# First layer of a conditioned Mamba block: places inside a chunk and halved pairs placed anew

## What is computed

```python
xn = layernorm(x) * (1 + scale) + shift            # scale, shift, gate from silu(cond) @ ada_w.T + ada_b
x_in, z = split(xn @ in_proj_w.T)                  # 1024 channels each
u = silu(causal_conv(x_in, 4 taps) + conv_b)
dt_r, B, C = split(u @ x_proj_w.T)                 # 64, 16, 16
dt = softplus(dt_r @ dt_proj_w.T + dt_proj_b)
h[t] = h[t-1] * exp(dt[t] * A) + dt[t] * u[t] * B[t]      # per channel, 16 states
y[t] = sum over states of h[t] * C[t]  +  u[t] * D
x1 = x + gate * ((y * silu(z)) @ out_proj_w.T)
```

## Time and profile before

| | us |
|---|---|
| median of 3 runs | 2549.21 (2546.92 to 2552.84) |
| the profiled execution, its time | 2547.39 |
| the profiled execution, its span | 2545.6 |
| mean granted clock of TensorE | 0.941 of full |
| first scan to last scan of the first layer | 81.7 to 2044.7 |

### The profile page before, as it was taken

The page is one execution under the profiler, slowest core; times in us unless marked ns, Lnnn a source line. Parts: engine busy times, 40 slices in busy tenths (PEclk is TensorE's granted clock), DMA queues, the critical chain, the costliest instruction groups (busy, mean ns, idle before and its releaser), DMA issues. The chain is left out here.

```text
span 2545.6 us, 23866 instructions
## 1 busy us (share of the span) xinstructions
PE 2240.3 (88%) x6820; PEld 1160.5 (46%) x6820; DVE 2241.4 (88%) x2508; ACT 1591.7 (63%) x3049; POOL 1879.0 (74%) x1217
## 2 busy tenths in 40 slices
PE   8798879887987898899878988898877899999999
PEld 3233334333433343334333433333333369988887
DVE  3789999999999999999999999999999976676656
ACT  3557756765676567657765776577555445556645
POOL 0699988988898889889998888899886742222325
PEclk9899989998998899899989998999898999999999
DMA  5510131032104100412041004110410211112113
GB/s 195 214 58 25 63 129 37 26 110 81 38 28 141 52 34 25 150 41 71 21 150 50 29 21 154 38 33 17 158 46 1 81 63 32 32 40 68 50 43 124
DMA packets 78049, 176.09 MB, mean 69 GB/s; under 512 B 7453, under 2 KB 10781, under 8 KB 77918
## 3 DMA queue, kind: packets, MB, share of 16 engines
q1 hardware_dynamic: 77918, 174.56, 19.8%
HBM read 157.23 MB, written 17.30 MB: 69 GB/s over the span
## 5 line engine op out<-in xcount | busy, mean ns | idle before, releaser
L1311 POOL TENSOR_TENSOR arena<-arena 128x1024 f32<-128x1024 f32 x512 | 1200.9, 2359 | 106.0 <-ACT arena L535 79.9
L929 DVE TENSOR_TENSOR_SCAN arena<-ps,arena 128x512 f32<-128x512 f32 x1024 | 1253.2, 1253 | 2.0 <-ACT ps L535 2.0
L535 ACT ACTIVATE ps<-arena 128x512 f32<-128x512 f32 x1088 | 730.5, 683 | 528.7 <-DVE arena L929 497.4
L300 PE MATMUL ps<-arena,keep 128*128 128x512 f32 x1712 | 867.8, 640 | 135.4 <-POOL arena L1311 69.6
L917 DVE TENSOR_TENSOR arena<-ps,arena 128x1024 f32<-128x1024 f32 x512 | 615.4, 1202 | 53.0 <-PE ps L300 39.7
L300 PEld LDWEIGHTS ps<-arena,keep 128*128 128x128 f32 x1712 | 340.0, 204 | 615.6 <-issue 386.8
L247 PE MATMUL ps<-arena 128*128 128x512 f32 x1024 | 464.6, 598 | 3.0 <-ACT arena L535 3.0
L247 PEld LDWEIGHTS ps<-arena 128*128 128x128 f32 x1024 | 197.8, 194 | 258.0 <-issue 255.0
L1276 POOL TENSOR_TENSOR arena<-arena 128x512 f32<-128x512 f32 x168 | 213.6, 1271 | 46.6 <-ACT arena L535 38.2
L286 PE MATMUL ps<-arena 128*128 128x512 f32 x512 | 232.9, 596 | 1.0 <-issue 1.0
L1316 POOL TENSOR_TENSOR arena<-arena 128x512 f32<-128x512 f32 x168 | 213.9, 1273 | 13.2
(11 more groups left out here) (130 smaller groups left out, 2607.7 us busy)
## 6 DMA issues: line engine op xcount, KB each, us to landing
arena<-scr_bc SPq DMA_DIRECT2D x128, 512.0 KB, 7.2
arena<-in_inT SPq DMA_DIRECT2D x128, 256.0 KB, 2.6
arena<-in_x SPq DMA_DIRECT2D x17, 512.0 KB, 3.7
scr_x<-arena SPq DMA_DIRECT2D x32, 256.0 KB, 2.0
arena_b<-scr_x SPq DMA_DIRECT2D x16, 512.0 KB, 3.6
arena_c<-scr_x SPq DMA_DIRECT2D x32, 256.0 KB, 2.8
out<-arena_c SPq DMA_DIRECT2D x32, 256.0 KB, 2.0
arena<-in_x SPq DMA_DIRECT2D x30, 256.0 KB, 3.2
```

What stands on the lines that cost most here:

```text
L300: last = e.matmul(YP, ident, hb[G % R][:, i, :], start=False, stop=(g == NG - 1 and i == n - 1))
L535: return e.activation(o_, i_, f, **kw)
L929: e.tensor_tensor_scan(H, DA[s % 4], H, h0, MUL, ADD).then_inc(v_sc)
L1311: m_ = e.tensor_tensor(H, H, Ct[:, GN * g:GN * g + GN, :], MUL)
```

## The change

It moves entries in the tables and writes the table of halved pairs anew; no step's own code changes. 168 pairs were halved; now it is 20 in each chunk but in unit 39 none, 157 in all. In a middle chunk: the output products go from slots 7, 8 of unit 0, 0, 3 of unit 1 and 3, 5, 9, 10 of unit 2 to slots 4, 8, 15 of unit 0, 5 of unit 1 and 3, 5, 9, 12 of unit 2. The input products x1 to x7 move by one to five slots, and their evacuations and taps with them. The second half of the norm's steps goes later, except RS, which goes earlier. `softplus` goes from slot 7 to 8, one `SILU` from (5, 11) to (5, 14), another, with `proj`, one slot later, and two z products later.

```diff
@@ -148,32 +148,32 @@
 
         after = lambda k, n: ((16 * k[0] + k[1] + n) // 16, (k[1] + n) % 16)
 
-        AT = {"dt": 4, "soft": 7, "add": 8, "du": 6, "copy": 13, "yf": 7, "proj": (6, 14), "xdbl": (7, 5)}
-        XMM = {(2, 12): 0, (3, 2): 1, (3, 15): 2, (4, 2): 3, (4, 11): 4, (5, 0): 5, (5, 15): 6, (6, 6): 7}
+        AT = {"dt": 4, "soft": 8, "add": 8, "du": 6, "copy": 13, "yf": 7, "proj": (6, 15), "xdbl": (7, 5)}
+        XMM = {(2, 12): 0, (3, 5): 1, (4, 1): 2, (4, 5): 3, (4, 13): 4, (5, 1): 5, (6, 0): 6, (6, 7): 7}
         XEV = {after(k, 4): i for k, i in XMM.items()}
         TAP = {after(k, (2, 3, 4)[w]): (i, 2 - w) for k, i in XMM.items() for w in range(3)}
-        SILU = {(3, 14): (0, 2), (5, 11): (2, 5), (6, 14): (5, 8)}
-
-        ZMM = {(1, 8): 1, (1, 10): 2, (3, 8): 1, (3, 10): 2, (5, 5): 1, (5, 10): 2, (7, 8): 1, (7, 12): 2}
-        ZSILU = {(1, 14): (1, 2), (3, 14): (1, 2), (5, 14): (1, 2), (7, 14): (1, 2)}
-
-        STATS = {(0, 3): 0, (1, 0): 1}
-        RS = {(0, 3): 0, (1, 6): 1}
-        NORM = {(0, 8): 0, (1, 11): 1}
-        NTR = {(0, 13): 0, (1, 13): 1}
-        NEV = {(0, 14): 0, (1, 15): 1}
-
-        OUTM = {(0, 7): 0, (0, 8): 4, (1, 0): 8, (1, 3): 12, (2, 3): 16, (2, 5): 20, (2, 9): 24, (2, 10): 28}
-        OUTA = {(0, 12): 0, (1, 3): 1, (2, 8): 2, (3, 1): 3}
-
-        HALF = {0: (2, 3, 4, 6), 1: (0, 1, 2, 3, 5), 2: (0, 3, 5), 3: (), 4: (4, 6), 5: (), 6: (5,), 7: (0, 2, 4, 5, 6, 7)}
+        SILU = {(3, 14): (0, 2), (5, 14): (2, 5), (6, 15): (5, 8)}
+
+        ZMM = {(1, 8): 1, (1, 10): 2, (3, 8): 1, (3, 10): 2, (5, 5): 1, (5, 11): 2, (7, 11): 1, (7, 12): 2}
+        ZSILU = {(1, 15): (1, 2), (3, 14): (1, 2), (5, 14): (1, 2), (7, 14): (1, 2)}
+
+        STATS = {(0, 0): 0, (1, 2): 1}
+        RS = {(0, 2): 0, (0, 15): 1}
+        NORM = {(0, 10): 0, (1, 5): 1}
+        NTR = {(0, 13): 0, (2, 1): 1}
+        NEV = {(0, 14): 0, (2, 3): 1}
+
+        OUTM = {(0, 4): 0, (0, 8): 4, (0, 15): 8, (1, 5): 12, (2, 3): 16, (2, 5): 20, (2, 9): 24, (2, 12): 28}
+        OUTA = {(0, 12): 0, (1, 6): 1, (2, 8): 2, (3, 1): 3}
+
+        HALF = {0: (5,), 1: (0, 1, 2, 3), 2: (0, 1, 2, 3), 3: (0, 1, 2), 4: (4,), 5: (3,), 6: (1, 5, 7), 7: (0, 2, 4)}
 
         CPART = {after(k, n): (i, n) for i, k in enumerate([(0, 6), (1, 6), (2, 2)]) for n in range(4)}
         CROW, CCOL, CEND = {(0, 11): 0, (1, 11): 1, (2, 7): 2}, {(1, 14): 1, (2, 9): 2}, {(2, 1): 1, (2, 12): 2}
 
-        GATE = {(1, 8): (0, 0), (1, 12): (0, 1), (2, 0): (0, 2), (2, 4): (0, 3), (39, 2): (1, 0), (39, 5): (1, 1),
-                (39, 8): (1, 2), (39, 11): (1, 3)}
-        halved = lambda U, g: g in HALF[U % 8]
+        GATE = {(1, 8): (0, 0), (1, 12): (0, 1), (2, 0): (0, 2), (2, 4): (0, 3), (39, 0): (1, 0), (39, 7): (1, 1),
+                (39, 9): (1, 2), (39, 15): (1, 3)}
+        halved = lambda U, g: g in HALF[U % 8] and U != 39
 
         WSEQ = [(0, i) for i in range(10)]
         for U in range(NU):
```

## The result

The changed kernel takes 2492.1 us (median of 4 runs, 2490.4 to 2493.1) against 2548.1 us for the kernel before on the same chip (median of 4, 2544.2 to 2552.8). The ratio is 0.978, 95% interval 0.976 to 0.980: 56 us faster. The profiled execution took 2492.05 us, its span is 2490.3.

A forecast was written before the change was run, and what follows sets the result against it. VectorE bounds the kernel; reordering can win only its 73.1 us idle in the first layer. Terms sum to -40 us: 2547.4 - 40 + 1.8 = 2509 us, range 2494 to 2543; the forecast case spans 2493 to 2524.

The forecast's parts named there:

- (4,6) and (5,6): Slot 6 of units 4 and 5: sums with 1.1 and 1.3 us to spare stall in a chunk or two, +2 us.
- unit 0, `expand` and `x1_add` at slot 12: Unit 0: both waits go at either clock, 2.3 us in each of 7 chunks, taken as -15 us.
- gates, units 39 to 41: Chunk 5: GpSimd has 29.5 us of work beside the gate products instead of 37.1, so waits go, -6 us.
- unit 6: TensorE's hole before `y_fin` shrinks from 3.8 us to about 2; if the clock stays high, -9 us.
- ScalarE's group: Unit 5: a silu moved to slot 14 delays the exps behind it, 0.3 us in 7 chunks, +2 us.
- seam: Before layer two's transposes: GpSimd ends 4 us sooner, TensorE has 3 matmuls more; 0 to 2 us, taken as -1.
- Unit 0 is the same: Unit 0: as in unit 6, TensorE idles (4.87 us), its sums run slowly, slot 12's `expand` idles 1.37 us.
- Rival C: Granted clock stays as it is, savings come back at other pairs, only the gates gain: 2543 us; chance 0.13.
- Rival A: Clock falls at a 3.1 us hole ending unit 3; units 4 and 5 lose 56 us: 2565 us; chance 0.09.
- Rival B: Clock falls at some of rival A's places or unit 6 stays low: 22 us gained, 2527 us; chance 0.20.
- Rival D: ScalarE's group exposed, 1.5 us in 7 chunks: 2518 us; with extra switch time 2536 us; chance 0.03 for both.
- the remaining 22 us: VectorE's idle time in units 3, 4, 5, 7 of seven chunks: half goes, -11 us, since spare is 1 us.

The follow-up runs named there:

- e2_places_only: The changed kernel with the old list of halved pairs in every unit, 39 included: 2517.6 us, ratio 0.989 to the kernel before.
- e5_fill016: The kernel before with four unread matmuls at slot 5 of units 0, 1 and 6: 2535.2 us, ratio 0.995.
- e10_fill1: The changed kernel with four unread matmuls at slot 5 of unit 1: 2494.5 us, ratio 0.979 to the kernel before.

## Why the prediction was right in sign and too small

The terms of the sum, us, by the two traces. The rows down to (4,6) and (5,6) are VectorE's idle time between the first and last scan, the unit rows without chunk 0:

| Step | forecast | measured |
|---|---|---|
| unit 0, `expand` and `x1_add` at slot 12 | -15 | -16.1 |
| unit 0, `expand` at slot 10 | 0 | -1.2 |
| gates, units 39 to 41 | -6 | -5.6 |
| unit 6 | -9 | -8.3 |
| units 3, 4, 5, 7 | -11 | -17.4 |
| a wait for a load in unit 1, and idle times under 0.15 us | 0 | -1.7 |
| chunk 0 | -2 | -4.5 |
| ScalarE's group | +2 | +1.3 |
| (4,6) and (5,6) | +2 | +1.4 |
| seam | -1 | -2.0 |
| overlap of VectorE's instructions | 0 | -3.9 |
| time to the first scan | 0 | +2.7 |
| sum (profiled spans 2545.6 and 2490.3) | -40 | -55.3 |

**Mechanism.** For unit 6 the chain from hole to clock to late sum to `expand` is shown, by unit 6 filled in the old order, and by chunk 2 against chunk 3 within the changed kernel. For unit 0 the order is what counts: its waits at slot 12 are gone in `e2_places_only` with the clock at 0.81 to 0.89, as the prediction said they would at either clock. "Unit 0 is the same" as unit 6 was wrong: the hole of 4.87 us ended at GpSimd's halving and not at `y_fin`. Rival C is out: the clock of unit 0 is 1.00 in chunk 3 and 0.94 to 1.00 in chunks 1 to 7. Rival A did not occur: the hole at the end of unit 3 is 1.7 us, not the 3.1 that I followed, the clock stayed high, and (4,6) and (5,6) cost 1.4 us outside chunk 0. Rival B is out, since the clock stayed high at all its places in most chunks (unit 6 kept it low in two). Rival D is out at both its prices: 1.8 us in all, chunk 0 included, in place of 10 or more. Nothing here shows the drain of about 1380 ns that the Trainium skill, ScalarE: Activation LUTs, section What ACT_TABLE_LOAD costs, adds to a switch: by it the moved group would have been exposed in every chunk, and the scan at (6,1) waits in three only. The load itself took 1.28 us, against the 1283 ns of the Trainium skill's page.

**The step that failed** is "the remaining 22 us ...: half, -11". By the traces these waits were 20.5 us and fell to 3.1, so -17.4; the other 1.8 of the 22 lay elsewhere. I took half because the spare was 1 us and I didn't follow these chains one by one. Most behaved all or none: (5,10) went from 8.0 to 0.9 us, `y_fin` at (4,7) and (5,7) from 7.7 to 0, `expand` at (4,0) from 2.5 to 0 (chunk 0 left out); only (7,4) kept 1.2 of its 1.6, and 0.9 came new at (4,10). For unit 5 my own numbers had said so: pair 7 is ready 2.5 us sooner against a wait of 0.9. That should have been taken whole.

**The low end of the range** was a wrong sum besides. "All but chunk 0's idle gone" is 73.1 - 14.5 = 58.6 us and not 56, so 2491 and not 2493.

**Terms that were missing.** Idle time was not "all that reordering can win". VectorE's busy time in the layer fell by 3.9 us (1889.9 to 1886.0) with the same instructions. In both kernels a scan that follows a scan without a wait starts 1190 ns after it, less than the recorded duration: neighbours overlap, and a wait loses that overlap besides its idle time. 46 waits fewer (72 to 26) for 3.9 us of busy time are 0.08 each. The other kernels fit roughly: busy 1884.1 to 1886.6 us with 20 to 36 waits, 1886.6 to 1889.6 with 43 to 61, 1890.5 with 90. Chunk 0 gave 2.5 us more than forecast, from its own units 4 to 6. Against it the first scan starts 2.7 us later; it lies between 79.8 and 85.3 us in the kernels here and I haven't found with what it goes.

**Costs taken as nothing.** `RS` at (0,15) was free, as said, and useful for a reason not seen. The gates' exception was worth nothing by itself; I had put the 6 us down to it.

**What was to be seen.** `x1_add` below 1 us, clock of unit 0, halvings and GpSimd's stand at (0,15): right. "A scan's mean is 1.25 us ... whatever the order" is not what the profile shows, 1302 ns now, but the pace is the same (see the end). Idle time 21 us for 30 to 36, chunks 1 to 7 of 234 to 242 for 240 to 242: more gain. "Chunk 5 no longer than the others" is wrong: at 241.5 us it is the longest of the middle ones, and it is one of the two whose unit 6 keeps the low clock; the other, chunk 2, takes 240.9, those with unit 6 at 1.00 237.4 at most. The seam is as forecast: GpSimd ends sooner, and TensorE's sums are last. The three engines at it, with the first transposes (L400) 9.4 us after the last scan and not 11.6:

```profile
1993.82 2.01 ACT L535 ACTIVATE wh_v<-arena_c 128x1024 fp32r<-128x1024 f32 x2 [5.64 <-POOL arena L1311]
1995.62 5.31 PE L300 MATMUL ps<-arena,keep 128*128 128x512 f32 x12
2000.77 1.04 PE L400 MATMUL ps<-keep,arena_b 128*128 128x128 f32 x8
```

## What to carry to other kernels

Look for the hole in which TensorE waits for a single buffer to be handed over, and read the granted clock behind it. Independent work put there paid in unit 6 even though it was work for nothing. Then look in the trace whether it really stands in the hole: behind it, or waiting for a bank of its own, it ran at the low clock and made the chain longer, as in unit 0 of `e5_fill016` and unit 1 of `e10_fill1`. Judge the places of the work and the load of the other engines region by region and together, since half of such a change can be slower than none. Where a wait is short against what a chain gains, count it as gone, not as halved.

## What the runs showed that I had not expected

28 unread matmuls, 24 us of TensorE's time on an engine busy 88% of the span, made the kernel 20 us faster. The recorded mean of VectorE's instructions is no measure of their cost: in the changed kernel a scan has 1302 ns and an `expand` 1248, in the kernel before and in the other runs 1249 to 1253 and 1196 to 1202, and yet scans in a row start 1190 to 1191 ns apart in all of them. A wait on VectorE costs about 0.08 us more than its idle time, by the two kernels compared here.
